# GpSimd's low part of `a` at the end of the turn, and layer-norm statistics in seven steps for eight, in a gated cross-attention block

## The chip, the cores and the metric

The kernel runs on one core of a Trainium2 chip. The metric is the device time of one execution in microseconds (us). The engines of the core are TensorE (PE in the profile, its weight loads PEld), VectorE (DVE), ScalarE (ACT), GpSimd (POOL) and SyncE (SP), whose queue issues the DMAs.

## What is computed

128 sequences of 128 tokens with 256 features. The block adds gated cross-attention with 16 heads of 16 features to `x`, and then a gated feed-forward part:

```python
x = x + tanh(g_xattn[0]) * xattn(values=ctx, keys=ctx, query=layernorm(x), mask)
x = x + tanh(g_ffn[0]) * tanh(layernorm(x) @ W @ A1 @ A2 + bias)

def layernorm(x):                    # over the 256 features, eps = 1e-5
    return (x - mean(x)) / sqrt(var(x) + eps)
```

Inside `xattn`, q, k and v are projections with biases, the scores are masked, scaled by 1/4 and put through a softmax over the keys, and the result is projected by `Wo`. All inputs and the output are float32. The three matrices of the feed-forward part are multiplied together once at the start.

## The kernel before

The 128 sequences are worked on in 64 pairs; a tile holds one pair, 128 partitions (tokens) by 2 x 256. Each engine has its program written out by hand, and semaphores tie them together. Each program is a loop over turns t = 0 to 63. The stages of one pair are spread over several turns: in turn t the engines normalise `x` of pair t + 2, project pair t + 1, compute the scores of pair t, divide the attention output of pair t - 3 by its denominators, project it by `Wo` for pair t - 4, and run the feed-forward part of pairs t - 5 and t - 6.

Each projection is done on operands that are split into a high part (ScalarE, a copy to a shorter format) and a low part (the rest: source minus high part). "Low part of `a`" is this subtraction for the divided attention output: `aT[:, 1] = a_norm - aT[:, 0]`.

GpSimd's turn, in the order of its queue, with the lines of the code:

- `low_of_ctx(t+1)` (414), waits for ScalarE's high part of the context
- `add_ffn_bias(t-6)` (431)
- `divide_a(t-3)` (420), makes `a_norm` and waits for the DMAs that bring `a_rows` and `den_wide`
- `finish(t-6)` (436) and `add_out_bias(t-2)` (410)
- `low_of_a(t-3)` (425), waits for ScalarE's high part (`aT_high`), signals `aT_ready`
- waits for VectorE's moments of `x` (pair t + 2) and of `y` (pair t - 4), then `rstd(t+2)`, eight small instructions on 128 x 4 values (369 to 383), each of which waits for the one before through the semaphore `ln_step`: variance plus eps, power -1/2, one Newton step, mean times reciprocal deviation, and its negative
- `normalise_x(t+2)` makes `xn`, `normalise_y(t-4)` makes `yn`, two instructions each (389)

TensorE's turn ends with `turn_x(t+2)` (line 490), which transposes `xn`. It waits for `k_ready` (ScalarE's four copies `k_aug`, line 773, of the keys of pair t + 1, because both use the PSUM tile `ps_m0`) and for `xn`. `make_f` (503) follows, and in the next turn the scores (603), `make_o` (503, reads `aT`), the transposed scores (624), the projections for q (496), v (565) and k (496). VectorE takes maxima (996) and masks (1007) between them.

SyncE's queue issues in this order within a turn, and each entry waits for what it needs:

```python
write_max(2 * t + 1)                      # line 324
if is_pair(t - 2):
    write_reciprocals(t - 2)
    read_a(t - 2)                         # a_rows, line 277
if is_pair(t - 4) and t - 4 <= END:
    write_y(t - 4)                        # waits for yn, line 293
read_max(2 * t + 1)                       # line 288, two DMAs
if is_pair(t - 2):
    read_wide(t - 2)                      # den_wide, line 258
```

What `read_wide(t-2)` brings is what GpSimd's `divide_a` uses in the turn after.

Of the kernel before, what the change touches and what calls it, by code (L numbers as in the profile page):

```python
# [10 lines left out]
ALU = mybir.AluOpType  # L11
# [19 lines left out]
def gated_xattn_block(nc, x, ctx, mask, g_xattn, g_ffn, Wv, bv, Wk, bk, Wq, bq, Wo, bo,  # L31
# [9 lines left out]
    with ExitStack() as stack:  # L41
        def sb(name, shape, dt=F32):
            return stack.enter_context(nc.sbuf_tensor(name, shape, dt))
# [4 lines left out]
        def sem(name):  # L48
            return stack.enter_context(nc.semaphore(name))
# [43 lines left out]
        ln_t = sb("ln_t", [P, 5, 2 * PAIR])  # L93
# [64 lines left out]
        ln_step, ln_v_step, x_step, y_step = sem("ln_step"), sem("ln_v_step"), sem("x_step"), sem("y_step")  # L158

        IDENT = 2  # L160
        RSTD = 8

        block = stack.enter_context(nc.Block())

        def wait(eng, semaphore, value):
            if value > 0:
                eng.wait_ge(semaphore, value)

        def is_pair(p):
            return 0 <= p < NP  # L170
# [14 lines left out]
        def flat(a):  # L185
            return a.rearrange("p a b -> p (a b)")
# [168 lines left out]
        @block.gpsimd  # L355
        def _(pool):
            for tile, value in ((c_eps, EPS), (c_minus_half, -0.5)):
                nc.gpsimd.memset(tile[:], value)
            nc.gpsimd.memset(ident[:], 0.0).then_inc(consts_ready, 1)
            pool.wait_ge(consts_ready, 1)  # L360
            nc.gpsimd.affine_select(out=ident[:], in_=ident[:], compare_op=ALU.not_equal, fill=1.0, base=0,
                                    pattern=[[-1, P]], channel_multiplier=1).then_inc(consts_ready, 1)

            def rstd(run):

                vp, r, a, b, nm = (ln_t[:, j, :] for j in range(5))
                moments = stat2[run % 2][:].rearrange("p a b z -> p (a b) z")
                mean, var = moments[:, :, 0], moments[:, :, 1]
                nc.gpsimd.tensor_tensor(vp, var, c_eps[:], ALU.add).then_inc(ln_step, 1)
                pool.wait_ge(ln_step, RSTD * run + 1)  # L370
                nc.gpsimd.tensor_tensor(r, vp, c_minus_half[:], ALU.pow).then_inc(ln_step, 1)  # L371
                pool.wait_ge(ln_step, RSTD * run + 2)
                nc.gpsimd.tensor_tensor(a, r, r, ALU.mult).then_inc(ln_step, 1)
                pool.wait_ge(ln_step, RSTD * run + 3)
                nc.gpsimd.tensor_tensor(b, a, vp, ALU.mult).then_inc(ln_step, 1)
                pool.wait_ge(ln_step, RSTD * run + 4)
                nc.gpsimd.tensor_scalar(a, b, -0.5, 1.5, ALU.mult, ALU.add).then_inc(ln_step, 1)  # L377
                pool.wait_ge(ln_step, RSTD * run + 5)
                nc.gpsimd.tensor_tensor(r, r, a, ALU.mult).then_inc(ln_step, 1)  # L379
                pool.wait_ge(ln_step, RSTD * run + 6)  # L380
                nc.gpsimd.tensor_tensor(a, mean, r, ALU.mult).then_inc(ln_step, 1)
                pool.wait_ge(ln_step, RSTD * run + 7)
                nc.gpsimd.tensor_scalar(nm, a, -1.0, None, ALU.mult).then_inc(ln_step, 1)
                pool.wait_ge(ln_step, RSTD * run + 8)

            def normalise(which, dst, src, ready):
                for i in range(PAIR):
                    j = which * PAIR + i
                    nc.gpsimd.tensor_scalar(dst[:, i, :], src[:, i, :], ln_t[:, 1, j:j + 1], ln_t[:, 4, j:j + 1],  # L389
                                            ALU.mult, ALU.add).then_inc(ready, 1)  # L390

            def normalise_x(p):
                wait(pool, xT_done, p)
                pool.wait_ge(x_landed[p % X_RING], 16 * (p // X_RING + 1))
                normalise(0, xn, x_in[p % X_RING], xn_ready)

            def normalise_y(p):
                if p <= END + 1:
                    wait(pool, yn_stored, 16 * p)
                else:  # L400
                    pool.wait_ge(yT_done, p - 1 - END)
                pool.wait_ge(y_ready, p + 1)
                normalise(1, yn, y[p % Y_RING], yn_ready)

            def add_out_bias(p):
                if p == 0:
                    pool.wait_ge(bo_ready, 1)
                pool.wait_ge(xn_ready, PAIR * (p + 1))
                tile = x_in[p % X_RING][:]
                nc.gpsimd.tensor_tensor(tile, tile, bo_wide[:].unsqueeze(1).to_broadcast([P, PAIR, E]), ALU.add).then_inc(x_biased, 1)  # L410

            def low_of_ctx(p):
                pool.wait_ge(cT_high, p + 1)
                nc.gpsimd.tensor_tensor(flat(cT[:, 1]), flat(ctx_T[:]), flat(cT[:, 0]), ALU.subtract).then_inc(cT_ready, 1)  # L414

            def divide_a(p):
                pool.wait_ge(a_landed, 16 * (p + 1))
                pool.wait_ge(wide_landed, 16 * (p + 1))
                wait(pool, aT_ready, p)
                nc.gpsimd.tensor_tensor(a_norm[:], a_rows[:], den_wide[:], ALU.mult).then_inc(a_norm_ready, 1)  # L420

            def low_of_a(p):
                pool.wait_ge(aT_high, p + 1)
                wait(pool, o_done, p)
                nc.gpsimd.tensor_tensor(flat(aT[:, 1]), a_norm[:], flat(aT[:, 0]), ALU.subtract).then_inc(aT_ready, 1)  # L425

            def add_ffn_bias(p):
                if p == 0:
                    pool.wait_ge(bf_landed, 16)
                pool.wait_ge(f_kept, p + 1)  # L430
                nc.gpsimd.tensor_tensor(th[:], th[:], bf_wide[:].unsqueeze(1).to_broadcast([P, PAIR, E]), ALU.add).then_inc(f_biased, 1)

            def finish(p):
                pool.wait_ge(th_gated, p + 1)
                tile = flat(y[p % Y_RING][:])
                nc.gpsimd.tensor_tensor(tile, tile, flat(th[:]), ALU.add).then_inc(res_ready, 1)  # L436

            nc.gpsimd.memset(neg_max[:], 0.0).then_inc(zeros_ready, 1)
            pool.wait_ge(stat1_ready, 1)
            rstd(0)  # L440
            normalise_x(0)
            nc.gpsimd.memset(ones_row[:], 1.0).then_inc(ones_ready, 1)
            nc.gpsimd.memset(v_ones[0][:].rearrange("p a b c -> p (a b c)"), 1.0).then_inc(ones_ready, 1)
            pool.wait_ge(stat1_ready, 2)
            rstd(1)
            normalise_x(1)
            for i in range(1, V_RING):
                nc.gpsimd.memset(v_ones[i][:].rearrange("p a b c -> p (a b c)"), 1.0).then_inc(ones_ready, 1)
            for t in range(NP):
                if t > 0 and is_pair(t + 1):  # L450
                    low_of_ctx(t + 1)
                if is_pair(t - 6):
                    add_ffn_bias(t - 6)
                if is_pair(t - 3):
                    divide_a(t - 3)
                if is_pair(t - 6):
                    finish(t - 6)
                if is_pair(t - 2):
                    add_out_bias(t - 2)
                if t == NP - 1:  # L460
                    add_out_bias(t - 1)
                    add_out_bias(t)
                if is_pair(t - 3):
                    low_of_a(t - 3)
                if is_pair(t + 2):
                    pool.wait_ge(stat1_ready, t + 3)
                if is_pair(t - 4):
                    pool.wait_ge(stat2_ready, t - 3)
                rstd(t + 2)
                if is_pair(t + 2):  # L470
                    normalise_x(t + 2)
                if is_pair(t - 4):
                    normalise_y(t - 4)
            for p in range(NP - 4, NP - 1):
                pool.wait_ge(stat2_ready, p + 1)
                rstd(p + 6)
                normalise_y(p)
            pool.wait_ge(ln_v_step, 1)
            nc.gpsimd.tensor_tensor(ln_v[:, 1, :], ln_v[:, 0, :], c_minus_half[:, 0:PAIR], ALU.pow).then_inc(ln_v_step, 1)
# [720 lines left out]
```

## Time and profile before

| | us |
|---|---|
| median of 3 runs | 1151.97 (1150.81 to 1156.32) |
| the profiled execution | 1147.69 |
| its span | 1145.9 |

The span is the part from the first to the last instruction; 1.8 us of the profiled execution lie around it.

| engine | busy us | share of the span |
|---|---|---|
| TensorE, matmuls | 1032.0 | 90% |
| TensorE, weight loads | 894.1 | 78% |
| VectorE | 954.2 | 83% |
| ScalarE | 831.6 | 73% |
| GpSimd | 797.5 | 70% |

Matmuls are pipelined and their ends are modelled, so that a busy TensorE is not one at its peak. The granted clock of TensorE is 9 tenths of full speed or more in all of 38 equal slices of the span and lower in the last two. The DMA engines are busy for about half of the time. In the chain of work that ended last, GpSimd holds 42% of the span, "issue" (no releaser seen) 27%, DMAs 10%, SyncE's queue 9%, TensorE 7%, VectorE 5%.

### The profile page before, as it was taken

How to read it: one execution, taken by the hardware profiler on the slowest of the kernel's cores; microseconds unless marked ns; L12 is line 12 of the kernel's file. 1: busy time of each engine (PE TensorE's matmuls, PEld its weight loads, DVE VectorE, ACT ScalarE, POOL GpSimd, SP SyncE). 2: the span in 40 equal slices, each digit the busy share in tenths (PEclk: the TensorE clock that was granted, in tenths of full speed). 3: DMA queues.
4: the chain of work that ended last, by engine and by line, in shares of the span. 5: the costliest groups of instructions: out<-in, count | busy, mean ns of one | idle time of the engine just before them, and what ended most of it. 6: DMA issues, size and time to landing. Idle time of an engine off the chain costs nothing.

```text
span 1145.9 us, 45278 instructions
## 1 busy us (share of the span) xinstructions
PE 1032.0 (90%) x18487; PEld 894.1 (78%) x18487; DVE 954.2 (83%) x1331; ACT 831.6 (73%) x1275; POOL 797.5 (70%) x1184
## 2 busy tenths in 40 slices
PE   5889999999999999999999999999999999999965
PEld 4768878888878877877887788888888788788855
DVE  5878888888888888888888888888888888888765
ACT  4466777777777777877777777777777777777742
POOL 5256677777767767777777777776777777777653
PEclk9999999999999999999999999999999999999987
DMA  5134455554555555545545555555555554554431
GB/s 146 42 111 124 129 154 144 148 153 134 161 144 146 149 140 145 153 137 150 149 137 156 143 147 151 144 151 147 146 145 145 144 153 136 149 150 126 125 126 66
DMA packets 260400, 158.87 MB, mean 139 GB/s; under 512 B 174945, under 2 KB 227170, under 8 KB 260194
## 3 DMA queue, kind: packets, MB, share of 16 engines
q1 hardware_dynamic: 260050, 155.72, 48.5%
q8 instruction: 147, 2.41, 0.9%
q14 instruction: 59, 0.48, 0.1%
q10 hardware_dynamic: 144, 0.26, 0.1%
HBM read 85.92 MB, written 68.94 MB: 135 GB/s over the span
## 4 chain that ended last, share of the span: by engine, by line
POOL 42%; issue 27%; DMA 10%; SPq 9%; PE 7%; DVE 5%; POOLq 0%; ACT 0%; DVEq 0%
DMA den_wide<-scratch_r 9%; POOL y L436 6%; POOL xn L389 5%; POOL aT L425 5%; POOL yn L389 5%; POOL ln_t L371 5%; SPq L288 5%; POOL x_in L410 5%; POOL ln_t L377 3%; SPq L293 2%; DVE probs L1007 2%; POOL ln_t L379 2%; DVE neg_max L996 2%; PE ps_s L603 1%; PE ps_s L624 1%
## 5 line engine op out<-in xcount | busy, mean ns | idle before, releaser
L996 DVE TENSOR_REDUCE neg_max<-ps_s 128x16 f32<-128x2048 f32 x128 | 293.2, 2291 | 71.2 <-PE ps_s L609 71.2
L1007 DVE TENSOR_TENSOR probs<-ps_s,far_T 128x2048 f32<-128x2048 f32 x128 | 291.0, 2273 | 27.7 <-PE ps_s L624 27.3
L798 ACT ACTIVATE probs<-probs 128x2048 f32<-128x2048 f32 x128 | 244.6, 1911 | 5.3 <-DVE probs L1007 4.9
L420 POOL TENSOR_TENSOR a_norm<-a_rows,den_wide 128x512 f32<-128x512 f32 x61 | 78.6, 1289 | 167.1 <-issue 163.6
L603 PE MATMUL ps_s<-k_aug,q_aug 32*128 32x128 f32 x4096 | 151.9, 285 | 17.4 <-DVE probs L1007 7.4
L603 PEld LDWEIGHTS ps_s<-k_aug,q_aug 32*128 32x128 f32 x4096 | 129.3, 188 | 38.1 <-issue 30.5
L624 PE MATMUL ps_s<-q_aug,k_aug 32*128 32x128 f32 x4096 | 151.1, 283 | 6.0 <-DVE neg_max L996 3.8
L624 PEld LDWEIGHTS ps_s<-q_aug,k_aug 32*128 32x128 f32 x4096 | 126.7, 186 | 23.6 <-issue 4.8
L635 PE MATMUL ps_x<-probs,v_ones 128*32 128x128 f32 x4096 | 138.9, 276 | 2.8 <-issue 2.0
L414 POOL TENSOR_TENSOR cT<-ctx_T,cT 128x512 fp32r<-128x512 f32 x62 | 79.1, 1276 | 85.2 <-ACT cT L748 85.2
L773 ACT ACTIVATE k_aug<-ps_m,k_bias,parity 128x256 f32<-128x256 f32 x256 | 123.5, 565 | 13.6 <-PE ps_m L496 13.0
L773 ACT ACTIVATE q_aug<-ps_m,q_bias,q_scale 128x256 f32<-128x256 f32 x256 | 122.7, 559 | 13.1 <-PE ps_s L624 7.2
L635 PEld LDWEIGHTS ps_x<-probs,v_ones 128*32 128x32 f32 x4096 | 104.3, 110 | 32.2 <-issue 32.0
L565 PE MATMUL ps_m<-wv_s,cT 128*128 128x256 f32 x756 | 117.8, 292 | 0.0
L748 ACT ACTIVATE aT<-a_norm 128x512 fp32r<-128x512 f32 x64 | 40.5, 633 | 104.8 <-POOL a_norm L420 97.9
L748 ACT ACTIVATE xT<-ps_m 128x512 fp32r<-128x512 f32 x65 | 38.9, 598 | 105.9 <-PE ps_m L490 103.3
L503 PE MATMUL ps_m<-wo_s,aT 128*128 128x256 f32 x768 | 110.6, 294 | 4.7 <-DVE aT L958 2.7
L503 PEld LDWEIGHTS ps_m<-wo_s,aT 128*128 128x128 f32 x768 | 97.5, 193 | 17.7 <-issue 15.6
L496 PE MATMUL ps_m<-cT,wk_s 128*128 128x256 f32 x768 | 109.2, 292 | 2.0 <-DVE wk_s L929 2.0
L503 PE MATMUL ps_m<-wf_s,yT 128*128 128x256 f32 x756 | 107.1, 292 | 3.5 <-DVE yT L958 3.5
L496 PE MATMUL ps_m<-xT,wq_s 128*128 128x256 f32 x768 | 108.1, 290 | 0.3 <-DVE xT L958 0.3
L496 PEld LDWEIGHTS ps_m<-cT,wk_s 128*128 128x128 f32 x768 | 96.2, 190 | 14.5 <-issue 11.7
(123 smaller groups left out, 1842.2 us busy)
## 6 DMA issues: line engine op xcount, KB each, us to landing
scratch_a<-a_den SPq DMA_DIRECT2D x64, 512.0 KB, 3.6
x_in<-in_x SPq DMA_DIRECT2D x64, 256.0 KB, 5.0
a_rows<-scratch_a SPq DMA_DIRECT2D x64, 256.0 KB
den_wide<-scratch_r SPq DMA_DIRECT2D x64, 256.0 KB
out<-y SPq DMA_DIRECT2D x64, 256.0 KB, 4.3
ctx_in<-in_ctx SPq DMA_DIRECT2D x252, 64.0 KB, 2.8
scratch_y<-yn SPq DMA_DIRECT2D x59, 256.0 KB, 3.2
y_blocks<-scratch_y SPq DMA_DIRECT2D x236, 64.0 KB
```

Of the source, the lines that this page charges most:

```text
L389: nc.gpsimd.tensor_scalar(dst[:, i, :], src[:, i, :], ln_t[:, 1, j:j + 1], ln_t[:, 4, j:j + 1], ALU.mult, ALU.add).then_inc(ready, 1)
L496: last = nc.tensor.matmul(dst[:, m * TOK:(m + 1) * TOK], w[:, a, k, m * P:(m + 1) * P], src[:, b, k, :], start=(n == 0), stop=(n == len(TE ...
L503: last = nc.tensor.matmul(dst[:, i * E:(i + 1) * E], src[:, a, k, i * P:(i + 1) * P], w[:, b, k, :], start=(n == 0), stop=(n == len(TERMS) ...
L565: last = nc.tensor.matmul(dst[:, i * E:(i + 1) * E], cT[:, a, k, i * P:(i + 1) * P], wv_s[:, b, k, :], start=(n == 0), stop=(n == len(TERM ...
L603: nc.tensor.matmul(ps_s[:, j, s, :], q_aug[p % 2][rows, n, s, :], k_aug[p % 2][rows, n, s, :], start=(s == 0), stop=False, tile_position=( ...
L624: last = nc.tensor.matmul(ps_s[:, j, s, :], k_aug[p % 2][rows, n, s, :], q_aug[p % 2][rows, n, s, :], start=True, stop=True, tile_position ...
L635: last = nc.tensor.matmul(ps_x[j * ROWS:(j + 1) * ROWS, s, :], v_ones[p % V_RING][:, n, h, :], probs[i % 2][:, j, s, :], start=True, stop= ...
L748: nc.scalar.activation(flat(dst[:, 0]), src, ACT.Copy).then_inc(ready, 1)
L773: last = nc.scalar.activation(dst[:, :, 2 * m + a, :], src[:, m * TOK:(m + 1) * TOK].rearrange("p (n q) -> p n q", q=P), ACT.Identity, bia ...
L798: nc.scalar.activation(tile, tile, ACT.Exp).then_inc(probs_ready, 1)
L996: nc.vector.tensor_reduce(neg_max[:, 0:H].rearrange("p (j c) -> p j c", j=G), ps_s[:], AX.X, ALU.max, negate=True).then_inc(max_ready, 1)
L1007: nc.vector.tensor_tensor(probs[i % 2][:].rearrange("p j s q -> p (j s) q"), ps_s[:].rearrange("p j s q -> p (j s) q"), far_T[:].unsqueeze ...
```

## The change

Three edits, all in GpSimd's program:

- `rstd` takes seven steps. Mean times reciprocal deviation goes into row 4 of `ln_t` (now `mr`), and the eighth step, which multiplied by -1, is gone. `RSTD`, by which VectorE's waits for `ln_step` are counted too, goes from 8 to 7.
- `normalise` subtracts: `src * r - mr` in place of `src * r + nm`.
- `low_of_a(t-3)` moves from in front of the waits for the moments to the end of the turn, behind `normalise_y`.

```diff
-        RSTD = 8
+        RSTD = 7
...
-                nc.gpsimd.tensor_tensor(a, mean, r, ALU.mult).then_inc(ln_step, 1)
+                nc.gpsimd.tensor_tensor(mr, mean, r, ALU.mult).then_inc(ln_step, 1)
                 pool.wait_ge(ln_step, RSTD * run + 7)
-                nc.gpsimd.tensor_scalar(nm, a, -1.0, None, ALU.mult).then_inc(ln_step, 1)
-                pool.wait_ge(ln_step, RSTD * run + 8)
...
                     nc.gpsimd.tensor_scalar(dst[:, i, :], src[:, i, :], ln_t[:, 1, j:j + 1], ln_t[:, 4, j:j + 1],
-                                            ALU.mult, ALU.add).then_inc(ready, 1)
+                                            ALU.mult, ALU.subtract).then_inc(ready, 1)
...
-                if is_pair(t - 3):
-                    low_of_a(t - 3)
                 if is_pair(t + 2):
                     pool.wait_ge(stat1_ready, t + 3)
...
                 if is_pair(t - 4):
                     normalise_y(t - 4)
+                if is_pair(t - 3):
+                    low_of_a(t - 3)
```

The last pair's `y` is normalised by VectorE with steps of its own (`normalise_last_y`), and those stay as they are.

## Rows read from the trace of the kernel before

**Rows 1.** Turns: window, length, busy PE, PEld, DVE, ACT, POOL, clock, DMA.
```profile
607.40:624.46 17.06, 15.77 (x288) 13.68 (x289) 14.85 (x21) 13.02 (x20) 12.67 (x19) 1.00 0.52 145
...
1066.31:1082.01 15.70, 15.64 (x289) 13.73 (x290) 11.91 (x16) 12.80 (x20) 11.23 (x16) 1.00 0.42 124
```
**Rows 2.** Waits from 132.37 to 1066.31: us in total, times, longest us.
```profile
PE ps_m L490 <- POOL xn L389: 61.3, 56, 1.5
```
**Rows 3.** Timeline of PE: start us, length us, line, operation.
```profile
115.01 0.66 PE L490 MATMUL ps_m<-ident,xn 128*128 128x128 f32 x4
...
268.05 0.63 PE L490 MATMUL ps_m<-ident,xn 128*128 128x128 f32 x4 [1.18 <-POOL xn L389]
...
607.40 0.63 PE L490 MATMUL ps_m<-ident,xn 128*128 128x128 f32 x4 [0.89 <-POOL xn L389]
...
609.38 1.17 PE L603 MATMUL ps_s<-k_aug,q_aug 32*128 32x128 f32 x32
...
611.86 1.69 PE L503 MATMUL ps_m<-wo_s,aT 128*128 128x256 f32 x12
...
619.70 1.69 PE L496 MATMUL ps_m<-cT,wk_s 128*128 128x256 f32 x12
```
**Rows 4.** Chain that ended last, from 600 us on: start, length, what.
```profile
608.35 0.38 SPq L293
...
609.97 1.87 DMA den_wide<-scratch_r
611.84 2.71 issue
```
**Rows 5.** Waits of the SP queue from 132.37 to 1066.31.
```profile
SPq L293 <- POOL yn L389: 92.3, 55, 2.4
```
**Rows 6.** Timeline of POOL, with idle time before and its releaser.
```profile
308.96 1.29 POOL L420 TENSOR_TENSOR a_norm<-a_rows,den_wide 128x512 f32<-128x512 f32 x1 [3.19 <-issue]
...
614.55 1.29 POOL L420 TENSOR_TENSOR a_norm<-a_rows,den_wide 128x512 f32<-128x512 f32 x1 [2.71 <-issue]
...
618.27 1.29 POOL L425 TENSOR_TENSOR aT<-a_norm,aT 128x512 fp32r<-128x512 f32 x1
619.53 0.20 POOL L369 TENSOR_TENSOR ln_t<-stat,c_eps 128x4 f32<-128x4 f32 x1
...
622.89 0.23 POOL L383 TENSOR_SCALAR ln_t<-ln_t 128x4 f32<-128x4 f32 x1
623.22 1.09 POOL L389 TENSOR_SCALAR xn<-x_in,ln_t 128x256 f32<-128x256 f32 x2
...
626.39 1.27 POOL L414 TENSOR_TENSOR cT<-ctx_T,cT 128x512 fp32r<-128x512 f32 x1 [1.00 <-ACT cT L748]
```
**Rows 7.** POOL's groups, 132.37 to 1066.31: shapes, count, busy us, mean ns, idle.
```profile
L425 POOL TENSOR_TENSOR aT<-a_norm,aT 128x512 fp32r<-128x512 f32 x55 | 71.1, 1292 | 0.0
...
L410 POOL TENSOR_TENSOR x_in<-x_in,bo_wide 128x512 f32<-128x512 f32 x55 | 70.1, 1274 | 0.0
...
L371 POOL TENSOR_TENSOR ln_t<-ln_t,c_minus_half 128x4 f32<-128x4 f32 x55 | 57.3, 1041 | 4.3
...
L373 POOL TENSOR_TENSOR ln_t<-ln_t 128x4 f32<-128x4 f32 x55 | 10.9, 198 | 4.3
```
**Rows 8.** Timeline of ACT, two turns.
```profile
113.03 1.93 ACT L773 ACTIVATE k_aug<-ps_m,k_bias,parity 128x256 f32<-128x256 f32 x4 [0.37 <-PE ps_m L496]
...
621.42 1.93 ACT L773 ACTIVATE k_aug<-ps_m,k_bias,parity 128x256 f32<-128x256 f32 x4 [0.24 <-PE ps_m L496]
```
**Rows 9.** Timeline of DVE, one turn.
```profile
617.76 0.25 DVE L1026 BATCH_NORM_AGGREGATE stat<-stat 128x2 f32<-128x6 f32 x2
...
622.56 2.29 DVE L1007 TENSOR_TENSOR probs<-ps_s,far_T 128x2048 f32<-128x2048 f32 x1 [0.37 <-PE ps_s L624]
```
**Rows 10.** Timeline of the SP queue, two turns.
```profile
267.81 0.60 SPq L277 DMA_DIRECT2D a_rows<-scratch_a  x1
...
302.29 0.38 SPq L293 DMA_DIRECT2D scratch_y<-yn  x1
```

More of the change, by code:

```diff
@@ L364, in rstd @@
             def rstd(run):
-                vp, r, a, b, nm = (ln_t[:, j, :] for j in range(5))
+                vp, r, a, b, mr = (ln_t[:, j, :] for j in range(5))
                 moments = stat2[run % 2][:].rearrange("p a b z -> p (a b) z")
```

## The prediction

> **What bounds the kernel now.** I read four views in this order: the busy time of the engines turn by turn, the list of waits, the chain that ended last, and the timelines of the engines laid side by side over one turn. A turn here is the time from one transposition of `xn` on TensorE (`turn_x`, line 490) to the next; I call its start T and the next one T'.
>
> The table by turn [rows 1] shows that from the turn at 607.40 on nobody is saturated: TensorE's matmuls are busy for 15.77 of 17.06 us, VectorE for 14.85, ScalarE for 13.02, GpSimd for 12.67, at a granted clock of 1.00 (2.4 GHz). The first turn of the end, which has all of the work but `turn_x`, took 15.70 us. The list of waits says who is late: TensorE waits 56 times for GpSimd's `xn`, 61.3 us in all, 1.09 us a turn [rows 2]. From T = 115.01 to T = 1066.31 there are 56 turns, one for each of these waits [rows 1 to 3], so a turn lasts 951.30 / 56 = 16.99 us. Nearly the whole loop lies in these turns.
>
> Why is `xn` late every turn? The chain [rows 4] is a ring through GpSimd, SyncE's queue and a DMA. SyncE issues its DMAs strictly in order. It waits for `yn` (92.3 us over 55 turns, [rows 5]), stores it, issues the two reads of the maxima and then the read of `den_wide`, and GpSimd's `divide_a` of the next pair waits for that. The reader is to see that everything GpSimd does between `a_norm` and `yn` delays the DMA that the next `a_norm` needs. The links, on the turn at 607.40: T to the store of `yn` 0.95 us (608.35), store to `a_norm` 6.20 us (614.55; 1.87 of it is shown as the DMA, 2.71 has no releaser in the trace) [rows 4, 6], `a_norm` to the first small step 4.98 us (619.53), small steps 3.69 us (623.22), `xn` and the pass to TensorE 1.24 us (624.46) [rows 1, 6]. The sum is 17.06 us, and it is the whole turn. The link that varies most is store to `a_norm`, which depends on DMAs: at its longest it took 6.67 us (302.29 to 308.96, [rows 6, 10]).
>
> **The change part by part.**
>
> Low part of `a` (line 425). It lasts 1.29 us and holds the queue from 618.27 to 619.53, 1.26 us of the ring [rows 6]. After the change it stands behind `yn`, outside the ring: neither `xn` nor the store of `yn` waits for it. Gain for the ring 1.26 us a turn.
>
> Eighth small step (line 383). From its start at 622.89 to the start of `xn` at 623.22 are 0.33 us [rows 6]; one wait of that kind remains, so I take 0.30. Gain for the ring 0.30 us a turn. The ring then takes 16.99 - 1.26 - 0.30 = 15.43 us.
>
> Subtract in place of add in the normalising instruction (line 389). The trace of before has no such form with a subtract. The nearest rows are tensor operations of one size that differ in the operation alone: the subtract of line 425 at 1292 ns, the add of line 410 at 1274 ns [rows 7]. That bounds it at 1.4% of 0.56 us on either side, about 0.01 us an instruction. The far end is the only operation on GpSimd in this kernel that does cost more by its kind, the power: 1041 ns where a multiply of that size takes 198 ns [rows 7], 0.84 us more. I take zero, since the row that is nearest is itself a subtract; the far end is a rival below. The result of the seventh step goes to another row of `ln_t` than before; that is the same instruction and costs nothing.
>
> What is late next. Taking the ring from 16.99 to 15.43 does not give 1.56 us, because `turn_x` also waits for `k_ready`: the transposition goes into the same PSUM bank (`ps_m0`) as the keys. ScalarE's four `k_aug` copies start at 621.42 and end at 623.35, that is T + 15.95 [rows 8], and they start as soon as the matmuls of the keys (from 619.70, [rows 3]) are through. They hang on T by TensorE's own stream, and GpSimd has no part in them. How soon `turn_x` follows them is seen in the one turn where `xn` was early: `k_aug` ended at 113.03 + 1.93 = 114.96, `turn_x` began at 115.01 [rows 3, 8]. So T' cannot be before T + 15.95 + 0.06 = T + 16.01. Held against each of the 56 turns (end of its `k_aug` copies plus 0.06, some of which are up to 0.2 us later), this second ring averages 16.03 us. It is longer than the first ring with its 15.43 us, so it becomes the bound, and of the 1.56 us only 0.96 us a turn arrive: 56 x 0.96 = 53.8 us, or 53.5 us by the sum over the single turns.
>
> Other rings that could be longer than 16.03. The statistics: GpSimd's steps now meet the wait for VectorE's moments sooner. These end at T + 10.61 (617.76 + 0.25, [rows 9]); with 3.69 - 0.30 us of steps and 1.24 us of `xn` that is T + 15.24. It lies 0.8 us under the bound. Before, the steps began 1.5 us after the moments, so this cover shrinks but is not gone; were it gone, each 0.1 us would cost 5.6 us in all. VectorE's own: its masking at 622.56 ends at T + 17.45 [rows 9], which would be T' + 1.44, and the next scores begin at T' + 1.98 (609.38 against 607.40 now), so it stays covered by 0.5 us.
>
> What is queued behind the moved instruction. On GpSimd, `low_of_ctx` of the next turn. With `xn` some 0.6 us ahead of its use, `yn`, which is stored at T + 0.95 now, ends near T' + 0.35, the low part of `a` near T' + 1.6. Now `low_of_ctx` begins at T + 1.93 because it waits for ScalarE (1.00 us of idle time stand before it, 626.39 against 624.46, [rows 6]), so it keeps its place. Who waits for the moved result: `make_o` on TensorE, which reads `aT` at T + 4.46 (611.86, [rows 3]). It has the result 9.4 us before now, and will have it 2.8 us before. I cost the move at nothing; if that cover were gone, TensorE would stand still before `make_o`. No DMA is issued from GpSimd here, and the wait for the high part of `a` (`aT_high`) moves with the instruction, to where it is long satisfied. Outside the 56 turns the small steps of the first two pairs and of pairs 60 to 62 lose 0.3 us each. Whether TensorE gains them lies between 0 and 5 x 0.3 = 1.5 us; I take none, since most of them end in front of other waits.
>
> SyncE's queue. In the new turn its work that hangs on TensorE comes 0.96 us later measured from T'. Now it is free for the store of `yn` by T + 0.36 in its latest turn (267.81 + 0.60 against 268.05), and in most turns 0.5 us or more before T [rows 3, 10]; then by T' + 1.32 at the latest, while `yn` is ready near T' + 0.35. So in some turns the store waits for the queue and not for GpSimd. At the latest, 1.32 + 6.20 + 3.72 + 3.39 + 1.24 = 15.87 us, still under 16.03; only together with the longest store-to-`a_norm` time (6.67) does it reach 16.34 and cost 0.3 us in that turn. I take 0.5 us for all turns.
>
> **The sum.** 53.5 - 0.5 = 53 us. The profiled execution took 1147.69 us (span 1145.9 and 1.8 around it) and becomes 1094.7. The median of the runs shown, 1151.97, lies 4.3 us above the profiled one; the same saving taken from it gives 1099.0. I predict 1099.
>
> A page of the Trainium skill judges TensorE otherwise. By busy matmuls it is at 15.77 of 17.06 us, which looks like little room; its weight loads are busy for 13.68 [rows 1]. The Trainium skill, Perfetto Trace Analysis, section Identifying the Most-Contended Engine, says that matmul busy time is no measure of the distance to the limit, since pipelined instructions look different in the trace, and that the busy share of LDWEIGHTS is one. By it TensorE would have room and GpSimd's ring would be the next bound, which is rival B below.
>
> **The rivals.**
>
> A. SyncE's queue becomes the bound. The issue of DMAs fills most of its turn, the wait for `yn` was its reserve (92.3 / 55 = 1.68 us a turn, [rows 5]), and some 1.0 us of it go. If the queue is as late in each turn as in its latest now, with the longest latency, the turn is 16.34 us: 56 x 0.65 = 36 us gained, 1116. For it: issues that take longer when the DMA queues are full push the queue back now already. Against it: most turns have the queue free before T.
>
> B. TensorE's stream closes up and the `k_aug` copies come earlier too, so that GpSimd's 15.43 us bind: 56 x 1.56 = 87 us, 1065; or, by the 15.70 us of the turn without `turn_x` [rows 1], 72 us, 1080. Against it: TensorE's only wait for GpSimd is the one before `turn_x` [rows 2], so nothing between T and the keys' matmuls at T + 12.30 can close up when GpSimd gets faster.
>
> C. Slower: the subtract form of the normalising instruction is slow on GpSimd. Four of them stand in the ring each turn. The ring has 16.99 - 15.43 = 1.56 us to spare until it is as long as before, so it decides from 0.39 us an instruction (0.56 to 0.95 us). With the price of the power, 0.84 us each, the turn is 15.43 + 3.36 = 18.79 us, 56 x 1.80 = 101 us slower, 1253. Against it: the subtract of two tensors costs what the add does [rows 7].
>
> D. No change: something that I don't see, released at the same time as `xn`, holds `turn_x`. 1152. Against it: `xn` ends 0.15 us before T' (623.22 + 1.09 against 624.46, [rows 6]), and the one turn in which it was early began 0.05 us after `k_aug`.
>
> **How the numbers follow.** Forecast 0.80, A 0.12, B 0.03, C 0.02, D 0.03. The forecast's own range: the saving between 50 and 55.5 us, taken from the profiled run or from the median, 1092 to 1102. The range that is to hold 8 in 10 reaches to A: 1091 to 1118; it leaves out B, C and D and what lies beyond A. Faster by over 0.5% (5.8 us, about what a measurement of this kernel can tell from no change): forecast, A and B, 0.95. Within 0.5%: D, 0.03. Slower: C, 0.02.
>
> **What the profile after would show.** Turns of 16.0 to 16.1 us on TensorE, `turn_x` 0.05 us after the end of `k_aug`, and its wait no longer put down to `xn` but to `k_aug` or to none. GpSimd's `xn` ends 0.5 us or more before T'; the idle time of GpSimd stands partly before line 369 (moments) and before line 414. The small steps take 3.3 us, seven of them. The low part of `a` runs between T' + 0.3 and T' + 1.7, and TensorE does not wait before `make_o`. SyncE's wait for `yn` falls from 1.7 to under 0.9 us a turn. The prediction is wrong if turns are of 16.3 us or more with `xn` still last (A), if `k_aug` ends before T + 15.9 (B), or if line 389 takes over 0.6 us (C).

## The result

The change makes the kernel slower. Median 1212.3 us (1206.7 to 1213.8) against 1151.9 us before, ratio 1.052 (95% interval 1.049 to 1.055). I had forecast 1099 us. The profiled execution took 1211.7 us with a span of 1209.9 us, 64.0 us more than the one of before.

The busy times on the page of the kernel after (us, share of the span, instructions). GpSimd has 69 instructions fewer than before, one small step in each of 69 passes, and is busy for 943.3 us where it was busy for 797.5:

```profile
PE 1058.3 (87%) x18487; PEld 917.3 (76%) x18487; DVE 957.5 (79%) x1331; ACT 831.4 (69%) x1275; POOL 943.3 (78%) x1115
```

Which instructions are they? GpSimd's groups of the kernel after, in all of its span (busy us, mean ns of one, idle time before). Lines are two lower than before from line 385 on: the normalising is line 387, the low part of `a` is line 423.

```profile
L387 POOL TENSOR_SCALAR xn<-x_in,ln_t 128x256 f32<-128x256 f32 x128 | 178.1, 1399 | 6.8 <-POOL ln_t L381 0.2
L387 POOL TENSOR_SCALAR yn<-y,ln_t 128x256 f32<-128x256 f32 x126 | 153.2, 1223 | 0.5
...
L423 POOL TENSOR_TENSOR aT<-a_norm,aT 128x512 fp32r<-128x512 f32 x61 | 77.8, 1276 | 0.0
```

The first two rows are what matters. The same instruction on the same tiles took 0.55 us with an add at the end, in the median and in almost every instance. These are its instances in the kernel before (shortest/median/longest ns):

```profile
L389 POOL TENSOR_SCALAR xn<-x_in,ln_t x128: 551/554/1122, 10.1 to 1065.6; 128x256 f32<-128x256 f32 x128
L389 POOL TENSOR_SCALAR yn<-y,ln_t x126: 548/556/1106, 98.4 to 1129.1; 128x256 f32<-128x256 f32 x126
```

In the kernel after the shortest and the median of `yn` are 1.21 and 1.22 us. Apart from a stall, told of below, the other instructions on GpSimd cost what they did.

The turns, with the columns of [rows 1]:

```profile
605.29:623.07 17.78, 15.78 (x288) 13.70 (x289) 14.61 (x20) 13.03 (x20) 15.03 (x18) 1.00 0.52 141
623.07:641.36 18.29, 15.81 (x288) 13.68 (x289) 14.61 (x20) 13.03 (x20) 15.03 (x18) 1.00 0.51 138
...
641.36:659.25 17.89, 17.27 (x288) 15.10 (x289) 13.63 (x20) 13.02 (x20) 14.52 (x18) 0.90 0.48 134
```

From 116.09 to 1131.95 the 56 turns average 18.14 us, 1.15 us more than before; 56 x 1.15 = 64.4 us is the whole difference of the two spans. `xn` is even later than before. The next two rows are TensorE's and the SP queue's waits in all of the span after, 93.1 and 182.4 us; over all of the span before, the same waits were 62.8 and 96.4 us ([rows 2, 5] give them for part of it):

```profile
PE ps_m L488 <- POOL xn L387: 93.1, 60, 2.2
```
```profile
SPq L293 <- POOL yn L387: 182.4, 59, 4.1
```

One turn of the kernel after, from T = 623.07 to T' = 641.36. First TensorE, then the SP queue, then GpSimd (start us, length us). They answer to [rows 3, 4, 6]:

```profile
623.07 0.63 PE L488 MATMUL ps_m<-ident,xn 128*128 128x128 f32 x4 [1.88 <-POOL xn L387]
...
627.53 1.69 PE L501 MATMUL ps_m<-wo_s,aT 128*128 128x256 f32 x12
...
641.36 0.78 PE L488 MATMUL ps_m<-ident,xn 128*128 128x128 f32 x4 [2.15 <-POOL xn L387]
```
```profile
625.36 0.39 SPq L293 DMA_DIRECT2D scratch_y<-yn  x1
```
```profile
625.30 1.27 POOL L423 TENSOR_TENSOR aT<-a_norm,aT 128x512 fp32r<-128x512 f32 x1
...
631.72 1.29 POOL L418 TENSOR_TENSOR a_norm<-a_rows,den_wide 128x512 f32<-128x512 f32 x1 [2.67 <-issue]
...
635.44 0.19 POOL L369 TENSOR_TENSOR ln_t<-stat,c_eps 128x4 f32<-128x4 f32 x1
...
638.25 2.96 POOL L387 TENSOR_SCALAR xn<-x_in,ln_t 128x256 f32<-128x256 f32 x2
641.20 2.41 POOL L387 TENSOR_SCALAR yn<-y,ln_t 128x256 f32<-128x256 f32 x2
```

It is still the ring of before, GpSimd to SyncE's queue to the DMA of `den_wide` to GpSimd. Its links, averaged over the 56 turns of each trace, in us ("store" is the issue of the DMA that stores `yn`):

| | T to store of `yn` | store to `a_norm` | `a_norm` to the first step | small steps | `xn` to T' | turn |
|---|---|---|---|---|---|---|
| before | 0.95 | 6.22 | 4.98 | 3.60 | 1.24 | 16.99 |
| after | 2.27 | 6.36 | 3.73 | 2.82 | 2.96 | 18.14 |

The third link lost 1.25 us, as the move was to do. The first and the last gained 1.33 and 1.72 us. That is where the four normalising instructions stand, two (`xn`) before T' and two (`yn`) around and behind T. The small steps lost more than their 0.30 us, and the last link gained more than 2 x 0.66 us. The reason for both is a stall of some 0.5 us, which comes once in most turns: it stood among the small steps before and stands in the first `xn` instruction now. That only moves it.

### The profile page after: what moved, and what is told of

It reads as the page before. It is cut to its first block, busy times and chain, and to the rows that moved or that the text cites. A ratio compares the mean times of both kernels' runs of the same rounds, so it can differ in the third digit from the quotient of the medians.

```text
span 1209.9 us, 45209 instructions
## 1 busy us (share of the span) xinstructions
PE 1058.3 (87%) x18487; PEld 917.3 (76%) x18487; DVE 957.5 (79%) x1331; ACT 831.4 (69%) x1275; POOL 943.3 (78%) x1115
## 4 chain that ended last, share of the span: by engine, by line
POOL 45%; issue 26%; DMA 11%; SPq 8%; PE 5%; DVE 4%; POOLq 0%; ACT 0%; DVEq 0%; ACTq 0%
POOL yn L387 12%; DMA den_wide<-scratch_r 10%; POOL xn L387 7%; POOL a_norm L418 6%; POOL ln_t L371 5%; SPq L288 5%; POOL x_in L408 5%; POOL y L434 4%; SPq L293 2%; DVE probs L1005 1%; PE ps_m L501 1%; DVE neg_max L994 1%; POOL ln_t L375 1%; POOL ln_t L373 1%; POOL ln_t L377 1%
## 5 line engine op out<-in xcount | busy, mean ns | idle before, releaser
L387 POOL TENSOR_SCALAR xn<-x_in,ln_t 128x256 f32<-128x256 f32 x128 | 178.1, 1399 | 6.8 <-POOL ln_t L381 0.2
L601 PE MATMUL ps_s<-k_aug,q_aug 32*128 32x128 f32 x4096 | 159.7, 295 | 14.3 <-DVE probs L1005 7.2
L601 PEld LDWEIGHTS ps_s<-k_aug,q_aug 32*128 32x128 f32 x4096 | 136.7, 198 | 36.6 <-issue 31.3
L387 POOL TENSOR_SCALAR yn<-y,ln_t 128x256 f32<-128x256 f32 x126 | 153.2, 1223 | 0.5
L501 PE MATMUL ps_m<-wf_s,yT 128*128 128x256 f32 x756 | 123.2, 321 | 3.6 <-DVE yT L956 3.6
L488 PE MATMUL ps_m<-ident,xn 128*128 128x128 f32 x256 | 41.7, 287 | 94.2 <-POOL xn L387 93.1
L494 PE MATMUL ps_m<-cT,wk_s 128*128 128x256 f32 x768 | 108.3, 291 | 11.5 <-issue 8.7
L501 PEld LDWEIGHTS ps_m<-wf_s,yT 128*128 128x128 f32 x756 | 110.7, 221 | 4.0 <-issue 4.0
```

Source lines behind the costliest of these rows:

```text
L494: last = nc.tensor.matmul(dst[:, m * TOK:(m + 1) * TOK], w[:, a, k, m * P:(m + 1) * P], src[:, b, k, :], start=(n == 0), stop=(n == len(TE ...
L501: last = nc.tensor.matmul(dst[:, i * E:(i + 1) * E], src[:, a, k, i * P:(i + 1) * P], w[:, b, k, :], start=(n == 0), stop=(n == len(TERMS) ...
L601: nc.tensor.matmul(ps_s[:, j, s, :], q_aug[p % 2][rows, n, s, :], k_aug[p % 2][rows, n, s, :], start=(s == 0), stop=False, tile_position=( ...
```

## The experiments

Two theories at the start. **S**: the subtract form of the normalising instruction costs 1.22 us where the add form costs 0.55, and nothing else hurts. **M**: the place of the low part of `a` hurts. The runs came in two groups of four, each timed beside the kernel before on its own chip: 1148.3 us (median) for the first four (the move alone, the other edits, the forms, and `make_f` first), 1150.9 us for the others. Ratios are to that.

### The move alone

```diff
-                if is_pair(t - 3):
-                    low_of_a(t - 3)
...
                     normalise_y(t - 4)
+                if is_pair(t - 3):
+                    low_of_a(t - 3)
```

> The kernel before with one edit of the change: GpSimd's low part of a moves behind the normalising of y; eight small steps and the add form stay. Theory S (the subtract form costs 1.22 us an instruction where the add form costs 0.55, and nothing else of the change hurts): the ring through GpSimd falls from 16.99 to 15.73 us a turn, the ring through the k_aug copies binds at 16.03 us, 56 turns x 0.96 us = 54 us faster than before, ratio 0.953; turn_x starts 0.05 us after k_aug ends. Rival M (the place of the low part of a is what costs, because low_of_ctx, the feed-forward bias and the tanh behind it are late): turns stay at 17 us or more, ratio 1.00 or above.

Measured: 1099.7 us, ratio 0.959 (0.956 to 0.961), 48.6 us less than before. M falls. The 56 turns average 16.12 us with a median of 16.04. Four views of this run: its waits, TensorE, ScalarE and GpSimd at one `turn_x`.

```profile
PEld ps_m L490 <- ACT k_aug L773: 23.0, 57, 1.2
...
PE ps_m L490 <- POOL xn L389: 1.5, 2, 1.0
```
```profile
633.06 0.66 PE L490 MATMUL ps_m<-ident,xn 128*128 128x128 f32 x4
```
```profile
631.08 1.93 ACT L773 ACTIVATE k_aug<-ps_m,k_bias,parity 128x256 f32<-128x256 f32 x4 [0.37 <-PE ps_m L496]
```
```profile
630.97 1.68 POOL L389 TENSOR_SCALAR xn<-x_in,ln_t 128x256 f32<-128x256 f32 x2
```

`xn` is ready at 632.65, `k_aug` at 633.01, `turn_x` starts at 633.06. TensorE's waits for `xn` went from 58 in the whole span to 2, and the copies took their place: in 55 of the 56 turns `turn_x` starts within 0.12 us of their end. The turn of 16.03 us is what the prediction had for them.

Five of the turns were 0.3 us or more above the median, one of them 17.78 us. In that one the read of `den_wide` was issued at 601.78 and `a_norm` began at 608.53, 6.75 us later and not the 4.6 us that it was before (609.97 to 614.55 in [rows 4, 6], and 4.57 us in the median of the 56 turns). ScalarE takes its work in order and waits for `a_norm`, so that all behind it in its queue, the `k_aug` copies at the end, was late too. From GpSimd's and ScalarE's timelines of this run:

```profile
608.53 1.27 POOL L420 TENSOR_TENSOR a_norm<-a_rows,den_wide 128x512 f32<-128x512 f32 x1 [4.67 <-issue]
```
```profile
609.90 0.63 ACT L748 ACTIVATE aT<-a_norm 128x512 fp32r<-128x512 f32 x1 [3.67 <-POOL a_norm L420]
```

The other four are of the same kind: from the issue of the read to `a_norm` they took 5.29 to 6.01 us, and all five end on the copies.

### The other edits alone

```diff
-        RSTD = 8
+        RSTD = 7
...
-                                            ALU.mult, ALU.add).then_inc(ready, 1)
+                                            ALU.mult, ALU.subtract).then_inc(ready, 1)
```

with `low_of_a` in its old place and the step that negates left out.

> The kernel before with the other edits of the change: seven small steps and the subtract form, the low part of a stays in its old place. Theory S: the ring through GpSimd is 16.99 - 0.30 + 4 x 0.66 = 19.33 us a turn, 56 x 2.34 = 131 us slower than before, ratio 1.114. Rival M (the move is what costs): at or under the time before, ratio 0.98 to 1.00.

Measured: 1283.0 us, ratio 1.119 (1.115 to 1.123), 135 us more. The turns average 19.40 us where S had 19.33. From the list of waits and the instances of line 387 (shortest, median and longest ns):

```profile
PE ps_m L488 <- POOL xn L387: 144.7, 61, 3.2
```
```profile
L387 POOL TENSOR_SCALAR yn<-y,ln_t x126: 1220/1227/1527, 98.3 to 1266.6; 128x256 f32<-128x256 f32 x126
```

The move takes 49 us off, the subtract form with its seven steps puts 135 us on. The sum would be 86 us, and the change measured 60. The move takes 1.26 us a turn off the ring, 71 us over 56 turns, of which only 49 can be had where the copies bind next. In the longer ring of the subtract form all of it counts: 19.40 - 1.26 = 18.14 us, the turn of the kernel after.

### What the forms cost by themselves

The kernel before, with 14 forms of `tensor_scalar` behind GpSimd's last instruction, three of each, each waiting for the one before:

```diff
+            for rep in range(3):
+                nc.gpsimd.tensor_scalar(b_dst[:, 0:256], b_src[:, 0:256], c1, c2, ALU.mult, ALU.add).then_inc(b_step, 1)
+                pool.wait_ge(b_step, 1 + rep * NF + 3)
+                nc.gpsimd.tensor_scalar(b_dst[:, 0:256], b_src[:, 0:256], c1, c2, ALU.mult, ALU.subtract).then_inc(b_step, 1)
+                pool.wait_ge(b_step, 1 + rep * NF + 4)
...
```

> The kernel before, and behind GpSimd's last instruction 14 forms of tensor_scalar, each three times, each waiting for the one before; they lengthen the kernel and their total time means nothing. Two column operands unless said: mult-add and mult-subtract on 64, 256 and 512 elements; on 256 elements subtract-mult, mult-mult, add-mult, mult-max, mult-add and mult-subtract with constants, one operation with a column operand: mult, subtract. Theory S1 (a subtract in any slot takes a slower path, by the element): mult-subtract is 0.55 + 0.66 us at 256 and the excess is 0.17 us at 64 and 1.3 us at 512; every form with a subtract is slow, the others take 0.55. Rival S2 (only the pair mult-add is fast, all else is slow): mult-mult, add-mult and mult-max take 1.2 us as well. Rival S3 (a fixed price of the form): the excess is 0.66 us at all three sizes.

The time of this run means nothing; it is the instances of each line that count (shortest/median/longest ns). In this order: multiply-add and multiply-subtract on 64 elements, multiply-add and multiply-subtract on 256, multiply-add and multiply-subtract on 512, then on 256 elements subtract-multiply, multiply-multiply, add-multiply, multiply-maximum, multiply-add and multiply-subtract with constants, one multiply, one subtract.

```profile
L488 POOL TENSOR_SCALAR b_dst<-b_src,ln_t x3: 387/388/397, 1129.3 to 1157.6; 128x64 f32<-128x64 f32 x3
L490 POOL TENSOR_SCALAR b_dst<-b_src,ln_t x3: 582/583/647, 1129.8 to 1158.1; 128x64 f32<-128x64 f32 x3
L492 POOL TENSOR_SCALAR b_dst<-b_src,ln_t x3: 554/555/561, 1130.5 to 1158.8; 128x256 f32<-128x256 f32 x3
L494 POOL TENSOR_SCALAR b_dst<-b_src,ln_t x3: 1218/1218/1754, 1131.2 to 1159.5; 128x256 f32<-128x256 f32 x3
L496 POOL TENSOR_SCALAR b_dst<-b_src,ln_t x3: 767/768/772, 1133.1 to 1160.8; 128x512 f32<-128x512 f32 x3
L498 POOL TENSOR_SCALAR b_dst<-b_src,ln_t x3: 2072/2073/2073, 1133.9 to 1161.7; 128x512 f32<-128x512 f32 x3
L500 POOL TENSOR_SCALAR b_dst<-b_src,ln_t x3: 1229/1229/1229, 1136.1 to 1163.8; 128x256 f32<-128x256 f32 x3
L502 POOL TENSOR_SCALAR b_dst<-b_src,ln_t x3: 556/556/559, 1137.4 to 1165.2; 128x256 f32<-128x256 f32 x3
L504 POOL TENSOR_SCALAR b_dst<-b_src,ln_t x3: 554/554/554, 1138.1 to 1165.8; 128x256 f32<-128x256 f32 x3
L506 POOL TENSOR_SCALAR b_dst<-b_src,ln_t x3: 1224/1224/1231, 1138.7 to 1166.5; 128x256 f32<-128x256 f32 x3
L508 POOL TENSOR_SCALAR b_dst<-b_src x3: 404/404/404, 1140.1 to 1167.8; 128x256 f32<-128x256 f32 x3
L510 POOL TENSOR_SCALAR b_dst<-b_src x3: 1074/1074/1074, 1140.6 to 1168.3; 128x256 f32<-128x256 f32 x3
L512 POOL TENSOR_SCALAR b_dst<-b_src,ln_t x3: 920/920/925, 1141.7 to 1169.4; 128x256 f32<-128x256 f32 x3
L514 POOL TENSOR_SCALAR b_dst<-b_src,ln_t x3: 922/922/922, 1142.8 to 1170.5; 128x256 f32<-128x256 f32 x3
```

The excess grows with the elements: from 64 to 512 elements multiply-subtract grows by (2.073 - 0.583) / 448 = 3.33 ns an element, multiply-add by (0.768 - 0.388) / 448 = 0.85 ns, so S3 falls. Among the forms of two operations the fast ones are those made of multiplies and adds alone (S2 falls: multiply-multiply and add-multiply take 0.55 us). A subtract is slow in either slot. But it is not the subtract only, as S1 had it: a maximum is as slow (1.22 us), and a form with a single operation takes 0.92 us whether that is a multiply or a subtract, more than a multiply and an add together. These two were timed at 256 elements only. The cause inside GpSimd isn't shown by these runs.

### Seven steps with a fast form

The list of forms offers another way to seven steps: (x - mean) * r as (x + minus mean) * r.

```diff
-        RSTD = 8
+        RSTD = 7
...
-                nc.gpsimd.tensor_tensor(a, mean, r, ALU.mult).then_inc(ln_step, 1)
+                nc.gpsimd.tensor_scalar(minus_mean, mean, -1.0, None, ALU.mult).then_inc(ln_step, 1)
                 pool.wait_ge(ln_step, RSTD * run + 7)
-                nc.gpsimd.tensor_scalar(nm, a, -1.0, None, ALU.mult).then_inc(ln_step, 1)
-                pool.wait_ge(ln_step, RSTD * run + 8)
...
-                    nc.gpsimd.tensor_scalar(dst[:, i, :], src[:, i, :], ln_t[:, 1, j:j + 1], ln_t[:, 4, j:j + 1],
-                                            ALU.mult, ALU.add).then_inc(ready, 1)
+                    nc.gpsimd.tensor_scalar(dst[:, i, :], src[:, i, :], ln_t[:, 4, j:j + 1], ln_t[:, 1, j:j + 1],
+                                            ALU.add, ALU.mult).then_inc(ready, 1)
```

First with the low part of `a` in its old place:

> The kernel before with seven small steps reached another way: the step that made mean times reciprocal deviation and the one that negated it give way to one that makes minus mean, and the normalising instruction is (x + minus mean) * r, add then multiply, which took 0.55 us among the forms measured. The low part of a stays in its old place. Theory S (only the slow form of the instruction spoiled the seven steps): the ring through GpSimd is 16.99 - 0.30 = 16.69 us a turn, 56 x 0.30 = 17 us faster than before, ratio 0.985. Rival F (another order of operands in the normalising costs something in this place too, or seven steps bring nothing): ratio 1.00 or above.

Measured: 1132.8 us, ratio 0.985 (0.982 to 0.987); the turns average 16.70 us against 16.69 expected. TensorE's wait for `xn` (62.8 us over the whole of the kernel before) falls to

```profile
PE ps_m L488 <- POOL xn L387: 45.2, 57, 1.2
```

which is 17.6 us less. The step is worth its 0.30 us a turn while GpSimd's ring is the bound.

Then the whole change in this form:

> The whole change with a fast form: low part of a moved, seven small steps, (x + minus mean) * r. Theory K (the k_aug copies bind at 16.03 us a turn): GpSimd's ring of 15.43 us has 0.6 us to spare, and the seventh step brings almost nothing beside the move alone: ratio 0.953 to 0.959, within 3 us of the move alone; most turns 16.03 us. Rival G (GpSimd's ring still sets the time in the kernel with the move alone): 17 us less than that, ratio 0.944.

Measured: 1099.8 us, ratio 0.957 (0.955 to 0.959), the same as the move alone. The median of the turns is 16.04 us again, and the wait list names the copies:

```profile
PEld ps_m L488 <- ACT k_aug L771: 24.5, 58, 1.2
```

Beside the move the step that is saved brings nothing that can be measured. The profiled execution was the slowest of the five, 1104.7 us, and its mean turn is 16.24 us: 10 turns were 0.3 us or more above the median, up to 18.08 us, and in all ten the read of `den_wide` took 5.1 to 7.2 us to the start of `a_norm`. All 56 turns end on the copies.

### One slow instruction beside the fast form

```diff
                 rstd(t + 2)
+                wait(pool, b_step, t)
+                nc.gpsimd.tensor_scalar(b_dst[:], ident[:, 0:64], ln_t[:, 1, 0:1], ln_t[:, 4, 0:1], ALU.mult,
+                                        ALU.subtract).then_inc(b_step, 1)
```

> As the whole change with the fast form, and one needless multiply-subtract on 64 elements (0.58 us, with its gap about 0.66 us) stands in front of the normalising of x in each turn; its result is used by nothing. It costs what one normalising instruction costs more in the slow form. Theory K: GpSimd's ring grows from 15.43 to about 16.09 us, 0.06 us over the bound of 16.03, so the kernel is only 3 to 8 us slower than with the fast form. Rival G (the ring is the bound throughout): 56 x 0.66 = 37 us slower.

Measured: 1105.2 us, ratio 0.961 (0.958 to 0.964), 5.4 us more than without it in medians, with intervals that overlap. That lies in the 3 to 8 us of theory K but isn't clear of noise. G, which had 37 us, falls. The two traces are closer still, 16.25 us a turn against 16.24. So 0.66 us, which would cost 37 us over 56 turns in the ring that binds, costs some 5 us or less where that ring has 0.6 us to spare. The wait for `xn` comes back 21 times:

```profile
PE ps_m L493 <- POOL xn L389: 13.7, 21, 1.0
```

### What stands behind the copies

TensorE does the feed-forward matmuls first and then the transposition, with the move alone:

```diff
                     else:
                         if is_pair(t + 1):
                             make_v(t + 1, 1)
-                        if is_pair(t + 2):
-                            turn_x(t + 2)
                         if is_pair(t - 5):
                             make_f(t - 5)
+                        if is_pair(t + 2):
+                            turn_x(t + 2)
```

> The move alone, and TensorE's make_f stands in front of turn_x, so that the 1.6 us of the feed-forward matmuls run while ScalarE ends the k_aug copies. Theory K (with the move alone the k_aug copies bind at 16.03 us a turn): turn_x no longer waits for them, and the turn falls to the longest of TensorE's own stream (15.70), VectorE's (15.6) and GpSimd's ring (15.73), about 15.75 to 15.8 us: 66 to 70 us faster than before, ratio 0.940 to 0.943, 14 us less than the move alone. Rival Q (SyncE's queue or GpSimd's ring bind in the kernel with the move alone): the same time as the move alone within 3 us.

Measured: 1100.4 us, ratio 0.959 (0.956 to 0.962). K, which had 66 to 70 us off, was wrong: it is 48. That is the time that Q had, but not for Q's reason. TensorE's waits for `xn` and for `k_aug` are down to three, 2.1 us in all. A new one takes their place, and the turns are of 16.14 us. First this wait and VectorE's for the high part of `x`, then TensorE and VectorE in one turn:

```profile
PE ps_s L624 <- DVE neg_max L996: 26.8, 59, 1.3
...
DVE xT L958 <- ACT xT L748: 59.7, 59, 1.6
```
```profile
623.21 1.17 PE L624 MATMUL ps_s<-q_aug,k_aug 32*128 32x128 f32 x32 [0.30 <-DVE neg_max L996]
```
```profile
619.40 0.69 DVE L958 TENSOR_TENSOR xT<-ps_m,xT 128x512 fp32r<-128x512 f32 x1 [0.79 <-ACT xT L748]
620.00 0.74 DVE L984 BATCH_NORM_STATS2 stat<-x_in 128x6 f32<-128x256 f32 x2
...
620.81 2.25 DVE L996 TENSOR_REDUCE neg_max<-ps_s 128x16 f32<-128x2048 f32 x1
```

VectorE takes its work in order. Before the low part of `x` it waits for a source that comes later now (59.7 us in all, where with the move alone it was 4.0 us), and the statistics and the maxima behind it are late. TensorE then waits for the maxima. The last run takes the statistics ahead of that wait and has the fast seven steps too:

```diff
-                if t > 0 and is_pair(t + 1):
-                    low_of_x(t + 1)
                 if is_pair(t + 3):
                     stats_of_x(t + 3, 0)
                     stats_of_x(t + 3, 1)
                 if t > 0 and is_pair(t + 2):
                     moments_of_x(t + 2)
+                if t > 0 and is_pair(t + 1):
+                    low_of_x(t + 1)
```

> As the one with make_f in front of turn_x, with the add-multiply form and seven steps, and VectorE takes the statistics of x before the low part of x, for which it waits for ScalarE. Theory V (with make_f first the turn of 16.14 us was bound by VectorE, which stood idle some 1.0 us before the low part of x and then came late with the maxima): the statistics fill that idle time, the turn falls to TensorE's own stream and VectorE's busy chain, 15.65 to 15.75 us, 56 x 0.4 = 22 us less than the move alone, about 1077 us, ratio 0.939. Rival W (some other ring of 16.1 us binds there): ratio 0.955 or above.

Measured: 1091.4 us, ratio 0.949 (0.947 to 0.951), the fastest of all, and between the 0.939 of V and the 0.955 of W. V is right in its mechanism: VectorE's wait for the high part of `x` falls to 11.4 us and TensorE's for the maxima to 2.2 us. It promised too much: 22 of the 56 turns are of 15.65 to 15.76 us, but the median is 15.86, and 13 are 0.3 us or more above that, so that the mean is 16.03. In 10 of these 13 TensorE waits for the reads of the maxima:

```profile
PEld ps_s L622 <- DMA q_aug<-scratch_m: 12.3, 14, 1.9
...
PE ps_s L622 <- DMA q_aug<-scratch_m: 8.5, 11, 1.7
```

In these 10 turns SyncE's queue was behind already: it issued the write of the maxima, which stands ahead of these reads, 0.7 to 2.0 us before T, and in the other turns 1.9 to 3.6 us before T. The seven steps came in with the same run and were not taken apart from the new order. `xn` was ready 1.4 us before its use in the run before it, so they had nothing to give through `xn`.

## Why the prediction was wrong

Step by step, as it was put.

**The bound before** was read rightly: the ring through GpSimd, SyncE's queue and `den_wide`. Both edits that shorten it gave what was worked out (1.25 us in the third link of the table, 0.29 us in 16.99 to 16.70). One reading was wrong: the longest time from the store to `a_norm` is not 6.67 us but 7.02, in the turn at 115.01.

**The low part of `a` behind `yn`** was right too. `make_o` does not wait for it: in the kernel after it is ready at 626.57 and read at 627.53, even with `yn` as late as it is there. What M feared is in that trace, ScalarE's tanh waits for the feed-forward bias behind the moved instruction, but ScalarE is busy for 13.03 of 18 us and has room for it. With the move alone there is no such wait. In the kernel after:

```profile
ACT th L813 <- POOL th L429: 31.1, 38, 0.8
```

**The next bound** was right: the `k_aug` copies, 16.03 us a turn, met by the move alone and by the whole change in its fast form. But I wrote that GpSimd has no part in these copies. In most turns it has none; in the late ones above it has, since ScalarE waits for `a_norm` ahead of them.

**Subtract in place of add** is the step that failed. I bounded it by the subtract and the add of two tensors [rows 7], which agree within 1.4%, took zero, and gave the slow form a chance of 0.02. These rows have the operation but not the form: they are another instruction (two tensors) and say nothing of how the one with column operands pairs its two operations. Measured, the subtract form costs 0.66 us more an instruction (1.22 us for 0.56), four times in each turn of the ring. With 0.66 us for 0.01 the working of rival C gives 15.43 + 4 x 0.66 = 18.07 us a turn, 56 x 1.08 = 60 us slower, 1208 us for the profiled execution; the measured turn is 18.14 us and the execution 1211.7. The point from which it decides, 0.39 us an instruction, was passed by 0.27. The sign that I gave for C, over 0.6 us for the normalising instruction, is what the profile shows.

**The range** named the far end (0.84 us, from the power) and then did not reach to it, because I gave that end its chance by the rows I had chosen for the near end. Four instances of an unseen form stood in the ring that binds; a row of that form was nowhere in the trace, and the chance should have been that of an unknown.

**SyncE's queue and late DMAs**, taken at 0.5 us for all turns, was too small. The mean turn of the move alone is 0.09 us over 16.03, 5 us in all, and it saved 48.6 us in medians, not 53. In the trace of the whole change in its fast form it is 0.21 us, 11.5 us in all; the median of its runs, 51 us below that of before, lies within my range. The late reads of `den_wide` above are of this kind. Why they take longer when the turn is shorter is not shown.

**The other rivals.** A (turns of 16.3 us or more with `xn` last) did not come: with the move alone, and in the whole change in its fast form, the late turns end on the copies and not on `xn`. D falls with the move alone, which is faster. B falls too, as all 56 turns of the whole change in its fast form end on the copies at a median of 16.04 us. With the copies off the path, what came next was VectorE's order (16.14 us), and behind that a median turn of 15.86 us with late reads in SyncE's queue. None of these is GpSimd's 15.43 us; 22 turns of the last run came near the 15.70 us that B had from the turn without `turn_x`.

## What to carry to other kernels

An instruction that changes one of its operations is a new instruction until a row shows it: price it by the same form with that operation, and where the trace has none, leave its full price in the range, times its instances in the ring that binds. When a ring is shortened, look for the next ring first and give the gain only down to that; here 1.56 us off gave 0.95 in the median turn. And an edit with a good effect can be hidden under one with a bad effect, so time them apart: the move alone is 4% faster than before, and the seven steps in their fast form alone 1.5%.

## What the runs showed of the hardware

GpSimd's `tensor_scalar` on float32 took 0.85 ns for each further element with multiply-add, and 3.33 ns with multiply-subtract. With two column operands and 256 elements: multiply-add, multiply-multiply and add-multiply 0.55 us against 1.22 us for multiply-subtract; subtract-multiply and multiply-maximum 1.23 and 1.22 us; one multiply or one subtract alone 0.92 us; with constants 0.40 and 1.07 us. A subtract of two tensors, in contrast, costs what an add does [rows 7].

The Trainium skill, GPSIMD Engine Reference, section Performance versus the Vector engine, gives 1.03 cycles an element for a body of up to two operations, and its section Specifications a clock of 1.2 GHz. That is 0.86 ns an element, an estimate from that page, which multiply-add meets (0.85 ns) and multiply-subtract, also of two operations, does not. The same page of the Trainium skill, section Performance pitfalls for Q7 kernels, gives 4 cycles an element for a dependent chain in float32; by the same clock that is an estimate of 3.33 ns, the number of the slow form. Whether such a chain is its cause, no run here shows.

A stall of about 0.5 us comes once in most turns on GpSimd, mostly in whatever instruction begins some 6.5 to 7.5 us after `a_norm` did: one of the small steps before (line 377 takes 0.50 us in the mean of the turns, and 0.20 us where no stall falls on it), an `xn` instruction in the kernel after and in the one with the move alone. It did not go away where the steps were fewer, and its cause stays open.

TensorE's granted clock was 1.00 (2.4 GHz) in all 56 turns before. In the kernel after it was 0.90 or 0.91 in the mean of 17 of the 56 turns. In the one that begins at 641.36 it lay at 0.50 (1.2 GHz) from 642 to 644:

```profile
642.00:644.00 2.00, 2.00 (x11) 2.00 (x11) 1.14 (x3) 1.11 (x2) 2.00 (x3) 0.50 0.08 31
```

Ahead of each of these 17 turns TensorE had stood still for 1.9 to 2.2 us; it had so ahead of others too, whose clock stayed at 1.00. In such a turn its matmuls are busy for some 17.3 us and not 15.8 (third row of the turns above), and the turn is no longer for it, 17.92 us in the mean against 18.24 for the others, since TensorE is not what binds.
